# Bilinear sampling rewritten: rows and row steps as stationary operands, one contraction tap inside each unit

## What is computed

```python
off = conv2d(x, ow, ob).reshape(Bn, K, 2, Hh, Ww)          # K = 9 taps
cy = iy + dy + off[:, :, 0]; cx = ix + dx + off[:, :, 1]
y0 = floor(cy); x0 = floor(cx); wy = cy - y0; wx = cx - x0
samp = gather(y0, x0, (1 - wy) * (1 - wx)) + gather(y0, x0 + 1, (1 - wy) * wx) \
     + gather(y0 + 1, x0, wy * (1 - wx)) + gather(y0 + 1, x0 + 1, wy * wx)
out = einsum('bckhw,ock->bohw', samp, w.reshape(O, Cin, K)) + b
...
h = relu(group_norm1(deform_conv(x, w1, b1, ow1, ob1), g1, be1)) + x
h = relu(group_norm1(deform_conv(h, w2, b2, ow2, ob2), g2, be2)) + h
```

## Time and profile before

| | |
|---|---|
| median of 3 runs | 748.67 us (747.22 to 749.94) |
| profiled execution | 753.67 us |
| its span, first to last instruction | 751.7 us |
| PE busy in the span | 593.7 us, 13258 matmuls and as many weight loads |
| DVE busy | 608.8 us |
| ACT busy | 489.6 us |
| mean granted TensorE clock | 0.896 |

### The profile page before, as it was taken

How to read it: one execution, slowest core, us unless ns; L and a number is a source line. 1 busy time by engine, 2 the same in 40 slices (tenths; PEclk the granted TensorE clock), 3 DMA queues, 4 the chain that set the end, 5 groups by cost and what they waited for, 6 DMA issues and landing times.

```text
span 751.7 us, 29125 instructions
## 1 busy us (share of the span) xinstructions
PE 593.7 (79%) x13258; PEld 417.2 (56%) x13258; DVE 608.8 (81%) x791; ACT 489.6 (65%) x736; POOL 150.6 (20%) x258
## 2 busy tenths in 40 slices
PE   2629999999886988888894977588888899386681
PEld 1216887766444766556672743467666666255350
DVE  6998999924279999999997425999999999785446
ACT  2876674233139899999974215879999998422514
POOL 1014000010452323444100143222344410000000
PEclk9959999999997899999997989889999999778696
DMA  5003000000798888888600269688888860000002
GB/s 208 0 23 93 3 4 19 4 3 23 202 324 293 265 311 277 263 262 257 256 4 2 54 173 370 235 288 279 268 263 252 265 241 2 3 3 3 2 3 113
DMA packets 30198, 111.16 MB, mean 148 GB/s; under 512 B 11140, under 2 KB 15940, under 8 KB 25976
## 3 DMA queue, kind: packets, MB, share of 16 engines
q0 software_dynamic: 14912, 87.85, 35.0%
q1 hardware_dynamic: 15160, 21.42, 9.5%
HBM read 92.25 MB, written 19.65 MB: 149 GB/s over the span
## 4 chain that ended last, share of the span: by engine, by line
PE 36%; DVE 30%; ACT 13%; DMA 9%; issue 7%; SPq 4%; POOL 0%; DVEq 0%; ACTq 0%; POOLq 0%
PE psum L1382 11%; PE psum L1436 6%; PE psum L1470 5%; DVE arena L809 5%; DVE arena L810 5%; PE psum L1585 4%; DVE arena L811 4%; DMA offsets<-arena 4%; DMA arena<-offsets_by_batch 3%; SPq L511 3%; ACT arena L1188 2%; ACT arena L1187 2%; ACT arena L1198 2%; ACT arena L1178 2%; PE psum L1592 2%
## 5 line engine op out<-in xcount | busy, mean ns | idle before, releaser
L1470 PE MATMUL psum<-arena 64*64 64x297 f32 (+4 forms) x4512 | 236.3, 357 | 44.8 <-DVE arena L811 29.2
L1470 PEld LDWEIGHTS psum<-arena 64*64 64x64 f32 x4512 | 176.5, 143 | 111.7 <-DVE arena L811 54.2
L1671 POOL DMA_DIRECT2D arena<-offsets_by_batch x128 | 82.5, 658 | 208.5 <-DVE arena L811 137.8
L1436 PE MATMUL psum<-arena 32*32 32x512 f32 x2304 | 90.9, 665 | 23.4 <-issue 17.5
L809 DVE SCALAR_TENSOR_TENSOR arena<-arena 128x792 f32<-128x792 f32 (+3 forms) x96 | 92.4, 962 | 5.7 <-ACT arena L1188 4.7
L1198 ACT ACTIVATE arena<-psum 128x792 f32<-128x792 f32 (+1 forms) x96 | 83.0, 865 | 20.3 <-PE psum L1470 11.4
L1382 PE MATMUL psum<-arena 32*32 32x512 f32 x2592 | 93.6, 597 | 0.0
L810 DVE SCALAR_TENSOR_TENSOR arena<-arena 128x792 f32<-128x792 f32 (+3 forms) x96 | 92.1, 959 | 0.0
L811 DVE SCALAR_TENSOR_TENSOR arena<-arena 128x792 f32<-128x792 f32 (+3 forms) x96 | 92.1, 959 | 0.0
L1188 ACT ACTIVATE arena<-arena 128x792 f32<-128x792 f32 (+3 forms) x96 | 84.7, 883 | 0.0
L1187 ACT ACTIVATE arena<-arena 128x792 f32<-128x792 f32 (+3 forms) x96 | 84.6, 881 | 0.0
(11 more groups left out here) (162 smaller groups left out, 691.6 us busy)
## 6 DMA issues: line engine op xcount, KB each, us to landing
arena<-offsets_by_batch POOLq DMA_DIRECT2D x112, 576.0 KB, 8.0
arena<-offsets_by_batch POOLq DMA_DIRECT2D x16, 624.0 KB, 7.7
offsets<-arena SPq DMA_DIRECT2D x32, 256.0 KB, 10.5
offsets_by_batch<-offsets SPq DMA_DIRECT2D x184, 24.0 KB
arena<-columns POOLq DMA_DIRECT2D x24, 160.0 KB, 9.6
columns<-arena POOLq DMA_DIRECT2D x8, 320.0 KB, 6.8
arena<-in_x SPq DMA_DIRECT2D x4, 512.0 KB, 5.4
out<-arena SPq DMA_DIRECT2D x8, 256.0 KB, 2.2
```

The costliest lines, as they stand in the source:

```text
L1436: ins = t_.matmul(ps_q(2 * axis + h, conv_bank(m) + i), cols(W_CONV[L] + (axis * K + t) * Q, Q, Q * i, Q), ap(XA + (BLK * m + 8 * h + t // ...
L1470: ins = t_.matmul(ps_t(s, bank + r, first * K * w, many * K * w), window, ap(g_at(unit, d0) + first * TW + s * w, [[GS + TW, many], [SLOTS ...
L1671: g.dma_start(cols(in_at(n, 0), 2 * in_rows(n) * W, 64 * r + 32 * half, 32), bass.AP(batch_d.tensor, 2 * (4 * r * NB + n) * INS, [[0, QW / ...
```

## The change

A sample is rewritten. Instead of three window rows with three tent weights, PE uses the tap's own row, weighted by the x tent alone, and the two steps between neighbouring rows (row + 1 minus row), weighted by max(y, 0) and min(y, 0) times the x tent. The sign of the x tent is turned at the end (`scale=-1.0` in the sample copy).

- DVE makes two products per unit instead of three, straight from the loaded y offsets. ACT's `y_terms` are gone.
- ACT spreads the rows themselves (`spread_rows`, four copies per batch); DVE subtracts neighbouring rows and spreads half of the steps, ACT the other half (`spread_steps`). The steps lie in a ring of nine rows; where a batch's four steps cross its end, each copy becomes two.
- PE has 5 step windows and 4 row windows per unit, 36 matmul calls instead of 24, with the loaded x tent itself as the moving operand of the row windows.
- The first of the two contraction taps of a unit goes inside the unit, ahead of its last step.
- The ring of 3 units holds two products per unit; the wait for PE moves from ACT's y terms to DVE's products. POOL's load waits for PE (`s_un`) instead of DVE (`s_g`).

```diff
-        s_zv, s_za = sem("window_rows_spread_by_vector"), sem("window_rows_spread_by_scalar")
+        s_za = sem("window_rows_spread_by_scalar")
+        s_dc, s_zv, s_zd = (sem("window_row_steps_ready"), sem("window_row_steps_spread_by_vector"),
+                            sem("window_row_steps_spread_by_scalar"))
...
-                    dve.wait_ge(s_nd, UNITS * L + unit + 1)
-                    v.scalar_tensor_tensor(term(0), term(0), 0.0, part(tx), ALU.min, ALU.mult)
-                    v.scalar_tensor_tensor(term(1), term(1), 1.0, part(tx), ALU.subtract, ALU.mult)
-                    v.scalar_tensor_tensor(term(2), part(ty), 0.0, part(tx), ALU.min, ALU.mult).then_inc(s_g, 1)
-                    if u == 1 and 1 <= n < NB - 1:
-                        spread_windows(L, n + 1)
...
+                    if unit >= RING:
+                        dve.wait_ge(s_un, UNITS * L + unit - RING + 1)
+                    v.scalar_tensor_tensor(term(0), part(ty), 0.0, part(tx), ALU.max, ALU.mult)
+                    v.scalar_tensor_tensor(term(1), part(ty), 0.0, part(tx), ALU.min, ALU.mult).then_inc(s_g, 1)
+                    if u == 1 and n + 1 < NB:
+                        spread_steps(L, n + 1)
+
+            def spread_steps(L, n):
+
+                c = n // 2
                 dve.wait_ge(s_zc[c % 2], 64 * (NCHUNK // 2 * L + c // 2 + 1))
+                dve.wait_ge(s_zd, NB * L + n)
                 dve.wait_ge(s_un, UNITS * L + NU * max(n - 1, 0))
...
+                ins = v.tensor_tensor(ap(DC, [[DCB, NBK], [C, rows], [1, C]]), row(1), row(0), ALU.subtract)
...
+                ins.then_inc(s_dc, 1)
+                dve.wait_ge(s_dc, NB * L + n + 1)
+                for i in range(2):
+                    for window, row_ in step_views(n, i):
+                        ins = v.tensor_scalar(window, row_, con("image4", i, 1), None, ALU.mult)
                 ins.then_inc(s_zv, 1)
...
-                    for i in (2, 3):
-                        ins = nc.scalar.activation(*spread_views(c, a, b, i), ACT.Copy, scale=con("image4", i, 1))
+                for i in range(4):
+                    ins = a.activation(*row_views(n, i), ACT.Copy, scale=con("image4", i, 1))
                 ins.then_inc(s_za, 1)
...
+            def spread_steps(L, n):
+
+                act.wait_ge(s_dc, NB * L + n + 1)
+                for i in (2, 3):
+                    for window, row in step_views(n, i):
+                        ins = a.activation(window, row, ACT.Copy, scale=con("image4", i, 1))
+                ins.then_inc(s_zd, 1)
...
-                    if unit + RING < UNITS:
-                        y_terms(L, unit + RING)
+                    if u == 0 and n + 1 < NB:
+                        spread_steps(L, n + 1)
                     if u == NU - 1 and n + 2 < NB:
+                        spread_rows(L, n + 2)
                         distances(L, n + 2)
-                        spread_windows(L, n + 2)
...
-                    for p in rows_:
-                        first = max(p - 1 - SLOTS * n, 0)
-                        d0 = first - (p - 1 - SLOTS * n)
-                        many = min(p + 1 - SLOTS * n, SLOTS - 1) - first + 1
+                    for p in range(-1, SLOTS):
+                        first, many = max(p, 0), 1 if p in (-1, SLOTS - 1) else 2
...
-                                window = cols(z_at(p, 2 * u + s), 64, 64 * r, 64)
+                                window = cols(d_at(SLOTS * n + p, 2 * u + s), 64, 64 * r, 64)
...
+                        if p < SLOTS - 1:
+                            for s in range(2):
+                                for r in range(2):
+                                    ins = t_.matmul(ps_t(s, bank + r, (p + 1) * K * w, K * w),
+                                                    cols(v_at(SLOTS * n + p + 1, 2 * u + s), 64, 64 * r, 64),
+                                                    ap(in_at(n, 0) + (p + 1) * W + u * TW + s * w,
+                                                       [[SLOTS * W, K], [1, w]], 64 * r, 64),
+                                                    start=False, stop=False, skip_group_check=True)
+                        if between and p == 2:
+                            j, tap = between
+                            contract(j, tap, tap + 1)
                     ins.then_inc(s_un, 1)
...
                 for unit in range(UNITS):
-                    sample(unit)
                     n, u = divmod(unit, NU)
                     step = NU * (n % 2) + u
                     if n >= 2 and 2 * step < K:
-                        contract(n // 2 - 1, 2 * step, min(2 * step + 2, K))
+                        sample(unit, (n // 2 - 1, 2 * step))
+                        if 2 * step + 1 < K:
+                            contract(n // 2 - 1, 2 * step + 1, 2 * step + 2)
+                    else:
+                        sample(unit)
...
                 if n >= 3:
-                    pool.wait_ge(s_g, UNITS * L + NU * (n - 2))
+                    pool.wait_ge(s_un, UNITS * L + NU * (n - 2))
```

More of the change, by code:

```diff
@@ L51 @@
 KP = 16
-ZROWS = 12
+VROWS = 2 * SLOTS
+DROWS = 2 * SLOTS + 1
 NCHUNK = NB // 2
-CHUNKS = [(8 * c + 1 if c else 0, min(8 * c + 9, H)) for c in range(NCHUNK)]
+CHUNKS = [(8 * c, min(8 * c + 9, H)) for c in range(NCHUNK)]
 CHUNK_ROWS = 9
@@ L203, in build @@
         G = IN_AT[2] + INK
-        YA = G + RING * 3 * GS
+        DB = G + RING * 2 * GS
+        ZROW = NBK * 64
+        YA = DB + DROWS * ZROW
         XA = YA + N
@@ L427, in g_at, with v_at, d_at, chunk_at @@
         def g_at(unit, d):
[L429 to L456, removed]
+            return G + (unit % RING * 2 + d) * GS
+        def v_at(row, blk):
+            return ZB + row % VROWS * ZROW + blk * 64
+        def d_at(row, blk):
+            return DB + (row + 1) % DROWS * ZROW + blk * 64
+        def chunk_at(n, row):
+            return ZC + n // 2 % 2 * ZCS + (row - CHUNKS[n // 2][0]) * C
+        def row_views(n, i):
+            return (ap(v_at(SLOTS * n, 0) + i * C, [[64, NBK], [ZROW, SLOTS], [1, C]]),
+                    ap(chunk_at(n, SLOTS * n), [[ZCB, NBK], [C, SLOTS], [1, C]]))
+        def step_views(n, i):
+            first = SLOTS * n
+            turn = min(SLOTS, DROWS - (first + 1) % DROWS)
+            views = [(ap(d_at(first + a, 0) + i * C, [[64, NBK], [ZROW, b - a], [1, C]]),
+                      ap(DC + a * C, [[DCB, NBK], [C, b - a], [1, C]])) for a, b in ((0, turn), (turn, SLOTS)) if a < b]
+            if n == 0:
+                views.append((ap(d_at(-1, 0) + i * C, [[64, NBK], [1, C]]), ap(chunk_at(0, 0), [[ZCB, NBK], [1, C]])))
+            return views
         def row_parts(bank, s, rho, y, rows):
@@ L1178, in distances @@
                 a.activation(tx, tx, ACT.Abs, bias=con("minus_q")).then_inc(s_u, 1)
-            def y_terms(L, unit):
-                n, u = divmod(unit, NU)
-                if unit >= RING:
-                    act.wait_ge(s_un, UNITS * L + unit - RING + 1)
-                part = ap(in_at(n, 1) + u * TW, [[W, in_rows(n)], [1, 2 * WB[u]]])
-                term = lambda d: ap(g_at(unit, d), [[TW, in_rows(n)], [1, 2 * WB[u]]])
-                a.activation(term(0), part, ACT.Copy, scale=-1.0)
-                a.activation(term(1), part, ACT.Abs).then_inc(s_nd, 1)
             def copy_samples(L, unit):
@@ L1224, in _ @@
                 distances(L, 0)
-                for unit in range(RING):
-                    y_terms(L, unit)
-                spread_windows(L, 0)
+                spread_rows(L, 0)
+                spread_steps(L, 0)
                 copy_offsets(L, 3)
+                spread_rows(L, 1)
                 distances(L, 1)
-                spread_windows(L, 1)
                 act.wait_ge(s_xs[0], 64 * (L + 1))
@@ L1450, in turn_columns, with sample @@
                     ins.then_inc(s_tp, 1)
-                def sample(unit):
+                def sample(unit, between=()):
                     n, u = divmod(unit, NU)
@@ L1472, in sample @@
                                                    [[GS + TW, many], [SLOTS * TW, K], [1, w]], 64 * r, 64),
-                                                start=(p == rows_[0]), stop=(p == rows_[-1]), skip_group_check=True)
-                                if (n, p) in ((0, 0), (NB - 1, H - 1)):
+                                                start=(p == -1), stop=(p == SLOTS - 1), skip_group_check=True)
+                                if edge:
                                     ins = t_.matmul(ps_t(s, bank + r, KR * w, 3 * w), window,
-                                                    ap(g_at(unit, 0 if n == 0 else 2) + KR * TW + s * w,
+                                                    ap(g_at(unit, 0 if n == 0 else 1) + KR * TW + s * w,
```

41 lines of the change are left out of this document (21 added, 20 removed).

## The result

The changed kernel takes **787.84 us** (median of 4 runs, 784.75 to 790.71) against 748.58 us for the kernel before beside it (4 runs, 747.22 to 749.94): a ratio of 1.0524, 95% interval 1.0471 to 1.0577. It is slower by 39.3 us. The forecast was 792, its range 732 to 815. The profiled execution took 785.65 us, its span is 783.7.

A forecast was written before the change was run, and what follows sets the result against it. DVE bounds sampling at 10.14 us per batch, then PE's instruction fetch at 11.8: 28 batches add 46.5 us to 753.67, giving 800; 795 at the runs' median, less 3 for the starts, 792 us. Range 732 to 815.

The forecast's parts named there:

- What bounds: Sampling, middle batches: DVE sets the pace before, 10.14 us per batch; after the change PE's instruction fetch does.
- DVE and ACT: Sampling, per batch: DVE falls from 10.14 to 8.1 us, ACT from 10.0 to 7.9 us.
- PE's columns: PE's sampling units: columns stay 1188 per array quarter, 12 more starts and weight loads cost nothing; 8.40 us per batch.
- Instructions: PE in sampling: 360 instructions per batch become 504, 1.97 blocks of 256; q8 brings about 124 packets.
- The price of a block: PE's fetch in sampling: 0 to 2.11 us per block over 4.27, so 8.4 to 12.6 us per batch, taken as 11.8.
- The reason for going below: PE's fetch in sampling: in some batches the second block is asked for between two loads, hence 11.8 us per batch.
- 28 batches: Batches 2 to 15 of each layer: 28 x (11.8 - 10.14) = +46.5 us; batches 0 and 1 counted as unchanged.
- 3 for the starts: The two sampling starts: some 3 us less, eight small ACT copies replacing six y terms before PE's first unit.
- The moved wait: POOL's batch load waits for PE, starting some 3 us later; over 20 us until use, against four issues and a landing.
- The tap ahead of the last step: PE's units: 4 calls move by one step, their samples copied more than a unit earlier; no cost added.
- The first rival: Sampling: fetch stays hidden, below 4.3 us in most blocks; 9.6 us per batch, 733 us in all; chance 0.25.

The follow-up runs named there:

- The control with quarter loads: Kernel before the change, each load of a batch's offsets cut to a quarter of its bytes: 743.45 us, ratio 0.9924.
- quarter loads: Changed kernel, POOL's batch loads of offsets cut to a quarter of their bytes, all 504 PE instructions kept: 695.73 us, ratio 0.9293.

## Why the prediction held, step by step

- **What bounds**: DVE set the batch before and PE's supply does after. Right. The control with quarter loads shows that the transfers did not bound the kernel before. In the changed one they do count, by the fetch and by the loads that PE releases.
- **DVE and ACT**: counted 8.1 and 7.9 us per batch. Over the six batches above DVE is busy 49.56 us and ACT 47.97, 8.26 and 8.00 each. Right.
- **PE's columns**: an uninterrupted batch of 8.30 us (counted 8.40), 8.60 with quarter loads. Right, and with it the price of nothing for the starts and weight loads of 12 more calls.
- **Instructions**: 124 packets, as forecast. Splitting the calls of the kernel before gives a loss of the same size. Right.
- **The price of a block**: taken as 11.8 us per batch. Where nothing but the instruction count was changed, in the kernel before with 36 calls, a batch takes 11.66 us. In the changed kernel, measured from the fourth batch on: 252.3 to 402.3 us in layer 0 and 517.0 to 660.6 in layer 1 are 12 batches each, 12.50 and 11.97 us, or 6.2 us per block: inside the own range of 10.5 to 12.6, and nearer to the 6.47 us of the convolutions than I had put it. The reason for going below, that some blocks ask between loads, agrees with the trace (14 stops for the 24 blocks that 150 / 12.23 batches of 1.97 make), but those that do stop make up for it, and the clock too: PE is busy 11 us in a stopped batch and 8 in the other.
- **28 batches**: this term was mis-sized the other way. The forecast had 28 x 1.66 = 46.5 us. Measured, the 24 batches cost 2.04 us more each by DVE's tents (12.23 against 10.20), 48.9 in all; the first three of each layer, 6.2 and 4.0 us shorter, give 10.1 back, where DVE's second and third gaps between tents are 7.9 to 9.5 us. That leaves 38.8 in the two samplings, and 6.8 are saved around them: 32.0 us between the profiled spans, where the forecast had 46.5 less 3 for the starts.
- **The moved wait**: called harmless with two batches' time. It was wrong by 6.5 us in the kernel before, and 45.2 us of ACT's time wait there in the changed one. The wait alone does not tell the cost: ACT waits 44.3 us there in the kernel with one call for the four rows too, at 736 us. The sum of two batches' time against four issues and a landing left out that the load closes a round from PE over POOL and ACT back to PE.
- **The tap ahead of the last step**: counted at nothing; it measures 7 to 9 us, and why is open. These two misses, some 13 to 16 us if they add, lie inside the measured batch, so the fetch's own part of it is less than 6.2 us per block; the split calls of the kernel before give 11.66 / 1.97 = 5.9. That the total came within 4 us of the forecast is so in part luck: the two terms counted at nothing made the batches dearer, and the starts and the stretches around the samplings gave back more than the 3 us counted.
- **The first rival**, the fetch hidden: 733 us at 9.6 per batch. The kernel with one call for the four rows is this case, 736 us at 9.92 and 10.16 us per batch. The number is close, the cause is another: not ACT's order behind the sample copy sets its batch, but the round through the loads, two batches in 19.9 us. With quarter loads, where neither fetch nor loads hold PE up, the batch is 8.60 us and the kernel 695.73: a batch of PE's 8.40 us was all but within reach. As far as these two kernels tell, the loads account for most of the 40 us between them.

## What to carry to other kernels

Count an engine's instructions like any other traffic: where a stretch of PE takes less time per 256 instructions than the fetch takes under its transfers, short calls cost what the columns do not show. Here four calls merged into one were worth 52 us, while the work taken off DVE and ACT gained nothing as long as PE stood still. The signs are stops named "issue" in the middle of a run, runs of the same number of instructions between them, and an instruction packet that lands just before each stop ends. Where the count can't fall, look at the loads that the fetch must pass, their length and when they start, and cut them only as far as the transfers keep their rate. When a wait is moved to another engine, follow the whole round that it closes: behind the fetch it was the loads released by PE that set the pace.

## What the runs showed of the hardware that was not expected

- The stops are no even tax. From 287 us on in layer 0 batches alternate between 8.30 us without a stop and 15.9 to 18.3 us with two. The loads, released by PE itself, come in pairs: POOL starts them at 287.84 and 295.76 us, then at 314.58 and 322.50, so that they fall on every other batch's blocks.
- A fetch is slow where loads fill the DMA engines. Behind PE's restart at 308.12 us, with few loads left, the next q8 packet starts 1.14 us later; behind the one at 298.15, with all 16 engines taken, 7.39 us later. Behind the stops between 250 and 400 us the longest such delay is 7.4 us with packets of 18432 bytes, 6.0 with the same packets spread out, 4.7 with 9216 bytes, and 2.7 and 5.9 in the two kernels with 4608 and the tap inside. The sums of the stops are 33.2, 28.9, 16.6, 6.6 and 12.9 us. They fall with the length of the packets, but that it is the cause is not shown: spreading the loads shortens the longest delay too, the kernels with 4608 bytes wait for loads as well, and with these the delay came out either way.
- Packets of 9216 bytes keep the rate (249 GB/s at a share of 0.76, against 218 at 0.72 with 18432); with sixteen loads of 4608 on two queues it falls to 216 GB/s at 0.83.
